# A gated two-pass attention: the first half's sum moved behind the second half's clip and the last query scaling on DVE

## The reference

```python
core = _gqa(q, k, v).reshape(b, s, nh * d)
...
xout = _gqa(qx, kx, vx).reshape(b, s, nh * d)
cat = jnp.concatenate([core, xout], axis=-1)
catq = _div_clamp_fp8(cat, proj_smooth)   # clip(x / scale, -448, 448) -> bf16 -> fp8 e4m3
return jnp.einsum('bsi,oi->bso', catq, wproj) * (proj_in_scale * proj_w_scale)
```

## Time and profile before

| | |
|---|---|
| median of 3 runs | 717.38 us (716.02 to 719.93) |
| profiled execution, its own time | 718.68 us |
| its span, first to last instruction | 717.0 us |
| busy, share of the span | PE 85%, DVE 71%, ACT 53%, POOL 51% |
| mean granted TensorE clock | 0.929 of 2.4 GHz |

### The profile page before, as it was taken

How to read it: one execution, slowest core, us unless ns; L and a number is a source line. 1 busy time by engine, 2 the same in 40 slices (tenths; PEclk the granted TensorE clock), 3 DMA queues, 4 the chain that set the end, 5 groups by cost and what they waited for, 6 DMA issues and landing times.

```text
span 717.0 us, 10737 instructions
## 1 busy us (share of the span) xinstructions
PE 607.7 (85%) x3738; PEld 487.4 (68%) x3738; DVE 511.7 (71%) x959; ACT 380.9 (53%) x674; POOL 366.0 (51%) x306
## 2 busy tenths in 40 slices
PE   4686986589677999999997898889888989999995
PEld 2453433353455888788876787778777878888885
DVE  4679777688259689888896688998998683533333
ACT  1445767765376465655575656665665424433321
POOL 2421265000367566565667766686775643755521
PEclk9897998789699899999998969999998999999999
DMA  7950211004502010010352031220220100221001
GB/s 234 309 198 0 104 73 59 31 36 156 162 11 79 1 60 30 30 61 0 118 198 84 29 113 50 74 69 22 74 74 16 45 1 1 67 66 31 1 1 59
DMA packets 36246, 50.68 MB, mean 71 GB/s; under 512 B 8289, under 2 KB 22497, under 8 KB 36193
## 3 DMA queue, kind: packets, MB, share of 16 engines
q1 hardware_dynamic: 36192, 50.00, 21.2%
HBM read 37.41 MB, written 12.58 MB: 70 GB/s over the span
## 4 chain that ended last, share of the span: by engine, by line
PE 41%; DVE 17%; issue 10%; ACT 3%; POOL 3%; DVEq 0%; POOLq 0%; ACTq 0%
PE g_proj L2077 7%; PE g_proj L2001 6%; PE g_scores L2035 4%; DVE g_yb L1623 4%; DVE g_ve L1591 3%; PE g_turn L2024 2%; PE g_proj L457 2%; PE g_proj L458 2%; PE g_proj L459 2%; PE g_op L472 2%; PE g_op L474 2%; PE g_op L473 2%; PE g_op L2059 2%; POOL g_rs L1495 2%; DVE g_big L1641 1%
## 5 line engine op out<-in xcount | busy, mean ns | idle before, releaser
L1495 POOL TENSOR_TENSOR g_rs<-g_ve,neg_half 128x4 f32<-128x4 f32 x96 | 101.9, 1066 | 85.1 <-DVE g_ve L1591 75.4
L1591 DVE TENSOR_REDUCE g_ve<-g_sq 128x4 f32<-128x516 f32 x96 | 64.3, 680 | 41.3 <-ACT g_sq L1807 32.9
L2001 PE MATMUL g_proj<-w_hi,g_xqc 128*128 128x512 f32 x192 | 85.7, 446 | 7.9 <-POOL g_xqc L1490 6.0
L1506 POOL TENSOR_TENSOR g_cat<-g_big,g_kb 128x1024 fp32r<-128x1024 bf16 x32 | 68.3, 2134 | 39.4 <-DVE g_big L1641 39.4
L2024 PE MATMUL g_turn<-ident,g_qn 128*128 128x128 f32 x384 | 60.5, 286 | 25.0 <-DVE g_qn L1597 15.0
L2001 PE MATMUL g_proj<-w_lo,g_xqc 128*128 128x512 f32 x192 | 79.9, 416 | 0.0
L1807 ACT ACTIVATE g_sq<-g_proj 128x512 f32<-128x512 f32 x80 | 47.8, 597 | 51.6 <-PE g_proj L2001 49.3
L2035 PEld LDWEIGHTS g_scores<-g_qkT 128*128 128x128 f32 x512 | 65.1, 205 | 12.4 <-issue 11.7
L2035 PE MATMUL g_scores<-g_qkT 128*128 128x64 f32 x512 | 66.1, 286 | 7.4 <-DVE g_ex L1607 7.4
L500 POOL TENSOR_TENSOR m_h_lo<-m_h,m_h_hi 128x512 fp32r<-128x512 f32 x32 | 41.3, 1294 | 59.8 <-ACT m_h_hi L487 59.8
L2024 PEld LDWEIGHTS g_turn<-ident,g_qn 128*128 128x128 f32 x384 | 46.2, 147 | 36.9 <-DVE g_qn L1597 17.5
(11 more groups left out here) (229 smaller groups left out, 1680.4 us busy)
## 6 DMA issues: line engine op xcount, KB each, us to landing
kvx_rows<-f_kept SPq DMA_DIRECT2D x32, 256.0 KB, 2.4
g_kraw<-kvx_rows SPq DMA_DIRECT2D x16, 256.0 KB, 3.3
g_v<-kvx_rows SPq DMA_DIRECT2D x8, 512.0 KB, 4.9
m_raw<-in_L_W SPq DMA_DIRECT2D x16, 256.0 KB, 3.3
c_raw<-in_L_wqT SPq DMA_DIRECT2D x4, 512.0 KB, 9.2
f_w_ctx<-in_L_wkvxT SPq DMA_DIRECT2D x4, 512.0 KB, 7.8
x_raw<-in_L_wqxT SPq DMA_DIRECT2D x4, 512.0 KB, 3.8
c_praw<-in_L_wprojT SPq DMA_DIRECT2D x4, 512.0 KB, 6.1
```

What stands on the lines that cost most here:

```text
L1495: G.tensor_tensor(rs[:, i % 2, :], ve[:, i % 2, :], k["half"][:, 0:4], ALU.pow).then_inc(q["rs_done"], 1)
L1506: G.tensor_tensor(cat[:, h].rearrange("p h (b s) -> p b h s", b=2), big[:, h, :].rearrange("p (b h s) -> p b h s", b=2, s=SEQ), kb[:, h, : ...
L1591: V.tensor_reduce(ve[:, i % 2, :], sq[:, i % 2], AX.X, ALU.add).then_inc(q["ve_done"], 1)
L2001: last = T.matmul(bank(n, i)[:], xqc[:, n % 2, view * KT + c_, :], w[:, c_, :], start=c_ == 0 and part == 0, stop=c_ == KT - 1 and part == 1)
```

## The change

In both rounds `lift(n, 0)`, DVE's sum of the first half, is moved behind the second half's `unload` and `clip` and the scaling of the last query chunk. The code of the last tile (outside both functions) stays as it is. Nothing else changes: the same instructions, the same semaphores and counts.

```diff
 # both_own(n), on DVE
                     power(n, 0)
                     scale(m, 4)
                     sums(m, 5)
-                    lift(n, 0)
                     unload(n, 1)
                     clip(n, 1)
                     scale(m, 5)
+                    lift(n, 0)
                     power(n, 1)
                     lift(n, 1)
...
 # both_cross(n), on DVE
                     clip(n, 0)
                     power(n, 0)
                     scale(m, 4)
-                    lift(n, 0)
                     unload(n, 1)
                     clip(n, 1)
                     scale(m, 5)
+                    lift(n, 0)
                     power(n, 1)
                     lift(n, 1)
```

## The result

The change made the kernel slower: 741.45 us (median of 6 runs, 737.64 to 743.72) against 717.90 us before (6 runs, 716.02 to 719.93) on the same chip. The ratio is 1.032, with a 95% interval of 1.029 to 1.036. The forecast was 730.4 us with a range of 718 to 742. Sign and mechanism came as forecast; the loss, 23.5 us, is nearly twice the 13 that I had summed. The profiled execution has a span of 740.8 us (before 717.0), so 23.8 us are to be found.

A forecast was written before the change was run, and what follows sets the result against it. No engine was full; a chain of waits between PE and DVE was taken as the bound. Order +4.1, five clock falls +12 and vanished falls -3 gave +13 on 717.38: 730.4 us, range 718 to 742.

The forecast's parts named there:

- DVE's side: In tile 4, the clip's stall moves to the second half's power pass; `less_max` starts 0.44 us later.
- The sum for order alone: Order on DVE and PE without the clock: own tiles +2.1 and context tiles +2.0, giving +4.1 us.
- the terms for rounds 7 to 13: Context tiles: 9 and 10 lose 1.1 us each, 7 loses 1.5, 12 about 0.7; 8, 11 and 13 together -0.9.
- the term for rounds 8, 11 and 13: Tiles where PE at half clock was later than DVE: an earlier turn gains, together -0.9 us, an estimate.
- 1.5 for round 14 and 1.7 for its clock: Tile 14: PE's wait for the turn is won, -1.5 us; one short clock fall goes, worth 1.7 us.
- five falls among the thirteen tiles 0 to 12: PE's longer single idle ahead of the second scores drops the clock five times at 2.4 us each: +12 us.
- the -3 for falls that go: Present clock falls partly lose their cause as the turn no longer waits: 1.7 in tile 14, 1.3 in other context tiles.
- three to eight falls: The forecast's own case, clock falls in tiles 0 to 12: 725 to 741 us, chance 0.56.
- the clock doesn't mind: Rival for the whole kernel: only order costs, +4.1 less up to 3, 719 to 722, taken as 721 us; chance 0.22.
- the clock falls in nearly every tile: Rival for PE's clock: 13 falls at 2.4 us, +32 in all, 750 us; chance 0.09.
- DVE keeps POOL out: Rival: both power passes run before POOL's difference, `less_max` starts 1.46 us earlier, -17, 700 us; chance 0.08.
- nothing changes: Rival: moved stall equals removed stall in each tile, tile 14 gains what tile 7 loses, 717 us; chance 0.05.

The follow-up runs named there:

- e3_fill: Changed kernel, but PE repeats a projection ahead of the second scores, filling its idle (once more in own rounds, twice in context rounds); 722.26 us, ratio 1.004.
- e4_last: Changed kernel with the first half's lift moved one step further, behind the second half's power too, in both rounds; 704.80 us, ratio 0.981.
- e2_context: Changed kernel with the new order only in the context rounds (7 to 14), the own rounds (0 to 6) keeping the old; 728.40 us, ratio 1.013.

## Why the prediction was right, and where its size was off

**DVE's side was right step by step.** From round 1 on the clip, forecast at 0.44 start to start, takes 0.43 us. The lift runs 0.61 behind the scaling. POOL's difference starts 0.16 behind the start of the mask pass (0.17 forecast) and is held up by 0.14 (2.26 for 2.12; 0.2 taken). The power pass stalls in all 15 changed rounds, 2.24 to 2.26 us where 2.2 to 2.5 was forecast, and ends 0.28 behind POOL. From the clip's start to `less_max` it is 4.91 us in round 4, forecast 5.06: the difference is the hold-up, and the scaling that begins 0.35 behind the clip's start instead of 0.44. The unloading itself begins 0.08 later behind the last sum of squares than the lift did before. That makes a loss of 0.29 in an even own round, not 0.44, and a gain of 0.06 in an odd one; the periods of `e3_fill` give 0.31 and 0.05. Round 0, where I had put the clip at 0.44 too, is the exception: its clip took 2.51 and its second lift 2.71, and it lost 0.68.

**The sum for order alone was too low, and the context rounds are where.** Forecast were +4.1. Measured is the span's 23.8 less the 17 of the clock, about 6.7; this remainder isn't measured by itself. Five own periods account for +0.8 (from `e3_fill`), where the steps gave +1.5. Between `less_max` of round 6 and that of round 14 it is +7.5 by the same subtraction, where the terms for rounds 7 to 13 gave +3.5. There `less_max` is reached 6.13 to 6.15 us after the unloading's start. Counted from the lift it was 5.21 in rounds 9 and 10 (+0.9, forecast +1.1) and 5.62 to 5.96 in the others. In rounds 7 and 8 the unloading waits for PE in both kernels, so that there the loss counts from the unloading, 4.87 before: +1.3 in each. So the term for rounds 8, 11 and 13, which I had taken as a gain of 0.9, had the wrong sign: by DVE's stretches they lost 1.3, 0.3 and 0.3. Behind the last `less_max` 2.0 us are won, where I had 1.5 for round 14 and 1.7 for its clock.

**The step that failed is "five falls among the thirteen tiles 0 to 12", and with it the -3 for falls that go.** The price was right: 78.5 us at half clock in 16 stretches is 4.9 each, so 2.45 us lost, and 1.5 or 3.1 by the periods. The numbers were wrong. Twelve falls are new, not five: eleven in rounds 1 to 13 and one in round 14. They have 54.6 us at half clock, so they cost 27 us, not 12. Against that, three falls are gone (13.7 us at half clock) and the four that stayed are 6.8 us shorter together, which gives back 10 us, not 3. Net it is 17 where I had 9. What I should have weighed higher is that in the own rounds every tile is like every other; once the piece of idle there was 1.76 us, the clock fell in all six of them.

That the time is still inside the range owes something to luck. With twelve falls at 2.4 and the rest as I had it, my sum would have come to +30, 747 us, outside; the larger give-back, which I hadn't foreseen, brought it to 741.45, just under the range's end of 742 and just above the 725 to 741 that I had given to three to eight falls.

**The rivals.** That the clock doesn't mind (721) falls with the measured ratio and with `e3_fill`: it is that kernel, with the same order but no wait of the second scores above 1.1 us from 242 us on, that lands at 722.3. The Trainium skill, "TensorE: Matmul & The Clock Gate", section "HAM oscillation", warns of idle gaps longer than the new waits of 1.75 to 2.69 us. Eleven of the thirteen rounds with such a wait had a fall all the same, which that warning doesn't cover, and the measurement decides.

That the clock falls in nearly every tile (750) was nearest in the count, twelve new falls for its thirteen. Its time is not what came, because it took back only 3 us for old falls, where the runs took back 10.

That DVE keeps POOL out falls with the power pass at 2.24. Its estimate, that `less_max` would start 1.46 earlier and the kernel take some 700 us, was nevertheless nearly the worth of such an order: `e4_last`, where the stalled passes run before POOL is released, took 704.8. That nothing changes falls with the ratio. The Trainium skill, "GPSIMD Engine Reference", section 1, says that POOL contends with DVE instructions in a two-port mode. No run here shows which mode a pass is in, but the pass that was next in line stalled as that rule would have it, 2.24 us for 0.43.

**What stays open.** Rounds 10 and 13 of the changed kernel had no fall although their scores waited as long as in others:

```profile
490.56 1.97 PE L2035 MATMUL g_scores<-g_qkT 128*128 128x64 f32 x16 [1.98 <-DVE g_ex L1607]
```

The scores there kept their 1.97 us behind 1.98 of idle. So a piece of 1.8 to 2.0 us was followed by a fall in most rounds but isn't always enough, and no run here tells what decides. In `e2_context` it is rounds 11 and 13 that had none, behind 1.99 and 1.98. The number of falls also differs between executions of one kernel: the 13 of the kernel before in one job took 714.80 to 723.91 us, with mean clocks from 0.941 down to 0.925. All counts above are those of one profiled execution each.

Nor does a run here separate the two things that the new order does to PE's idle. It joins two pieces, and it makes their sum longer (1.26 to 1.76 us in an even own round, 1.58 to 1.77 in an odd one). `e3_fill` takes away both.

## What to carry to other kernels

A bf16 pass of DVE that stands still beside a POOL operation isn't freed by moving the operation that releases POOL, if another such pass then starts beside it: the stall goes there. The two need not share data; in round 0 it is the centring of a weight that holds up the clip. Move the releasing operation behind all such passes, and split the wait of the consumer so that POOL's lateness isn't paid in one place. And count not only how much idle a reordering gives PE but also how long its longest piece becomes: here 9.5 us more idle, now in one piece per tile, came with 34 us more at half clock, which cost more than the idle.

## What the runs showed that I had not expected

In the kernel before, pieces of 0.80 and 0.46 us (even own rounds) and of 1.14 and 0.44 (odd ones) left the clock at 2.4 GHz through rounds 1 to 6, though `e2_context` had two short falls at the latter. A single piece of 1.76 or 1.77 was followed by a fall in each of these six rounds; one of 0.87 (`e3_fill`) by none. Work that computes nothing new, 21 us of it, laid into PE's idle made the changed kernel 19 us faster, and the same work in a place without idle made the kernel before 19 us slower. And the wait that was expected to eat the gain of `e4_last` came to 0.7 us in a tile, because the operations ahead of it began earlier as well.
